# Two attention quads a pass over the array, rows through HBM, and the input norm on ScalarE, in a transformer sandwich on one core

## The reference

```python
def _taylor_softmax(x):
    t = 1.0 + x + 0.5 * x * x
    return t / jnp.sum(t, axis=-1, keepdims=True)

# _L0_attn_ref(x, ln_w, ln_b, w_q, w_kv, w_o, theta)
h = (x - mu) * jax.lax.rsqrt(var + EPS) * ln_w + ln_b
q = h @ w_q
kv = h @ w_kv
q, k, v = (to_heads(q), to_heads(k), to_heads(v))
q = _rope(q, theta); k = _rope(k, theta)
qk = jnp.einsum('bhkd,bhqd->bhkq', q, k) * scale
attn = _taylor_softmax(qk)
wv = jnp.einsum('bhkq,bhqd->bhkd', attn, v)
return wv.transpose(0, 2, 1, 3).reshape(B, T, DIMS) @ w_o

# _L0_ffn_ref(x, weight, bias): input and weight are rounded to a 6-bit grid, scaled by blocks of 32
xq, xs = _mx_quantize(x2)
wq, ws = _mx_quantize(w2)
out = xd @ wd.T + bias

# the whole
x = x + _layernorm(_L0_attn_ref(_layernorm(x, axis=-1), ...), axis=-1)
x = x + _layernorm(_L0_ffn_ref(_layernorm(x, axis=-1), ...), axis=-1)
```

## Time and profile before

| | |
|---|---|
| median of 3 runs | 648.65 us (647.7 to 649.6) |
| profiled execution | 651.11 us |
| its span, first to last instruction | 648.8 us |
| TensorE busy | 615.9 us, 95% |
| VectorE busy | 594.8 us, 92% |
| ScalarE busy | 530.0 us, 82% |
| GpSimd busy | 449.3 us, 69% |
| granted TensorE clock, mean | 0.985 |

### The profile page before, as it was taken

One profiled execution on the slowest core, in us unless ns is written; L12 is line 12 of the kernel. 1 busy time (PEld: TensorE's weight loads), 2 busy tenths in 40 slices (PEclk: granted clock), 3 DMA queues, 4 the chain that ended last, 5 costly groups with the idle time before them and its releaser, 6 DMA issues. The chain is left out here.

```text
span 648.8 us, 20724 instructions
## 1 busy us (share of the span) xinstructions
PE 615.9 (95%) x6620; PEld 457.7 (71%) x6620; DVE 594.8 (92%) x1489; ACT 530.0 (82%) x1448; POOL 449.3 (69%) x785
## 2 busy tenths in 40 slices
PE   6889999999999999999999999999999999999974
PEld 5666667676776776777777777767777766788763
DVE  5799899899899989999999999989999999987796
ACT  4347788888788897989888888978888888999973
POOL 3475466677777878788777867767877777765464
PEclk9699999999999999999999999999999999999996
DMA  7101031222223232232323232223223212230201
GB/s 245 34 2 42 20 76 30 72 63 65 50 72 88 70 91 68 75 84 67 62 67 83 77 86 73 69 57 101 60 68 92 76 39 41 68 91 18 68 26 49
DMA packets 52362, 43.51 MB, mean 67 GB/s; under 512 B 7201, under 2 KB 48545, under 8 KB 52257
## 3 DMA queue, kind: packets, MB, share of 16 engines
q1 hardware_dynamic: 51440, 41.42, 24.1%
q10 hardware_dynamic: 816, 0.79, 0.4%
HBM read 18.65 MB, written 8.39 MB: 42 GB/s over the span
## 5 line engine op out<-in xcount | busy, mean ns | idle before, releaser
L1168 ACT ACTIVATE feat<-ps_f 128x512 f32<-128x512 f32 x256 | 144.4, 599 | 4.9 <-PE ps_f L852 4.3
L691 DVE TENSOR_TENSOR kf<-kf 128x896 f32<-128x896 f32 (+1 forms) x128 | 131.2, 1027 | 1.8
L852 PE MATMUL ps_f<-qT,selr 128*128 128x512 f32 x320 | 122.1, 435 | 1.8 <-ACT qT L1236 1.3
L691 POOL TENSOR_TENSOR kf<-kf 128x224 f32<-128x224 f32 x64 | 76.5, 1195 | 13.3 <-DVE kf L1515 11.1
L1015 PEld LDWEIGHTS ps_mt<-kf,vp 128*32 128x32 f32 x2048 | 64.1, 110 | 30.0 <-issue 28.3
L1015 PE MATMUL ps_mt<-kf,vp 128*32 128x153 f32 x2048 | 79.7, 296 | 0.6 <-DVE kf L691 0.6
L1725 POOL TENSOR_TENSOR qsp<-kf,qsp 128x256 fp32r<-128x256 f32 x64 | 58.6, 916 | 9.8 <-ACT qsp L1259 9.6
L852 PEld LDWEIGHTS ps_f<-qT,selr 128*128 128x128 f32 x320 | 52.8, 190 | 15.2 <-issue 11.0
L913 PE MATMUL ps_o<-feat,main 120*32 120x512 f32 x448 | 59.7, 604 | 0.0
L916 PE MATMUL ps_o<-feat,rm 128*32 128x512 f32 x448 | 58.6, 593 | 0.0
L788 PE MATMUL ps_qk<-wkqv_h,hT_l 128*128 128x512 f32 x128 | 52.4, 409 | 3.3 <-DVE wkqv_l L1425 3.3
(11 more groups left out here) (199 smaller groups left out, 1885.2 us busy)
## 6 DMA issues: line engine op xcount, KB each, us to landing
xc<-L_attn_x SPq DMA_DIRECT2D x16, 512.0 KB, 4.5
result<-fin SPq DMA_DIRECT2D x64, 128.0 KB, 2.0
xa<-L_attn_x SPq DMA_DIRECT2D x15, 512.0 KB, 4.1
heads_out<-osb SPq DMA_DIRECT2D x224, 32.0 KB, 2.0
shares<-sums SPq DMA_DIRECT2D x112, 64.0 KB
sums<-osb SPq DMA_DIRECT2D x224, 2.0 KB
wkqv<-L_attn_w_kv ACTq DMA_DIRECT2D x2, 256.0 KB, 4.9
xa<-L_attn_x SPq DMA_DIRECT2D x1, 384.0 KB, 6.2
```

Source lines behind the costliest of these rows:

```text
L691: return eng.tensor_tensor(dims(row, F_MAIN, [[FW, heads], [HD, NR - 1], [1, HD]]), dims(row, F_LIN, [[FW, heads], [0, NR - 1], [1, HD]]), ...
L852: pe.matmul(ps_f[i % 2][:, :], selr[:, i], queries, start=True, stop=True).then_inc(sel_done, 1)
L1168: act.activation(feat[:, p2, i], ps_f[i % 2][:, :], ACT.Square).then_inc(squared, 1)
```

## The change

Five things are changed together.

- **Two quads at once.** `attend` now runs once for two quads, into two banks: `ps_o` and `ps_w`. The blocks that serve four heads are built from other columns of q (`fold_kq` puts them in another order): the fifth block of a quad now holds two heads of each of two quads, one quad in rows 0 to 63 and the other in rows 64 to 127. The products with `rm` are 64 rows deep instead of 128, those of one quad with the upper and those of the other with the lower half of the rows and in another bank. There are still four for a quad. `feat` still holds two tiles, which one pair now fills, so the first squares of a pair wait for the `attend` of the pair before. The linear layer moves from bank `ps_w` to bank `ps_qk`, which the projection of q and k also uses.
- **Rows through HBM.** `move_pair` writes two quads of `osb` to a buffer `rows` in HBM with one DMA; once both pairs are there, `fetch_heads` reads the denominators back with one and the heads with two; `store_inverses` writes the inverses with one, and `spread_shares` reads them with two. That is 8 DMAs a sequence (2, 3, 1 and 2) instead of 40.
- **The input norm on ScalarE.** `normalise_x` goes from VectorE to ScalarE; it needs `-mean/deviation`, which GpSimd makes in one more instruction a tile (`shift_x`).
- **Small ones.** `constant` and `rest_terms` are split in two stages each (`sum_linear`, `scale_terms`), with the same instructions. The turned weight of the linear layer goes through `ps_tr`.
- **A new order** for every engine, and 17 fillers (`fill`, two small matrix products of constants each) on TensorE in steps 1 to 47.

```diff
-    "tensor": (58, {
-        "attend": ((43, 54, 65, 76, 90, 101, 114, 127, 140, 154, 168, 183, 198,), (25, 39, 53, 69,), (474, 489, 503,
...
+    "tensor": (56, {
+        "attend": ((53, 72, 98, 123, 145, 170,), (38, 66,), (373, 402, 430, 459, 486, 515, 541, 567, 598, 622, 654, 682,
...
-        ps_o = bank("ps_o")
+        ps_o = [bank("ps_o"), ps_w]
...
-        rm = sb("rm", [P, 2, NQ, P])
+        rm = sb("rm", [P, 2, CH, HQ, VW])
...
+        rows = nc.dram_tensor("rows", [2, NQ, P, T], F32).ap()
+        inverses = nc.dram_tensor("inverses", [H * T // P, P], F32).ap()
...
-            def move_quad(t):
+            def move_pair(t):
 
-                par, quad, s = t.par, t.tile, t.seq
-                if quad == 0:
-                    wait(sp, norm_ready, NT * (s - 1))
-                    for tile in range(NT):
-                        wait(sp, shares_in[tile], 16 * CH * s)
+                par, quads = t.par, slice(t.tile - 1, t.tile + 1)
+                wait(sp, heads_in[par], 16 * CH * (t.load - 1))
+                wait(sp, sums_in, 16 * (t.seq - 1))
                 sp.wait_ge(o_copied, t.n)
-                for part in range(NT):
-                    sp.dma_start(sums[part * H + HQ * quad:part * H + HQ * (quad + 1)],
-                                 osb[HD:P:VW, par, quad, part * P:(part + 1) * P]).then_inc(sums_in, 16)
-                for h in range(HQ):
-                    row = HD * (HQ * (quad % 2) + h)
-                    sp.dma_start(heads_out[row:row + HD, par, quad // 2], osb[VW * h:VW * h + HD, par, quad]).then_inc(heads_in[par], 16)
+                sp.dma_start(rows[par, quads].rearrange("q r n -> r q n"), osb[:, par, quads]).then_inc(moved[par], 16)
+
+            def fetch_heads(t):
+
+                par, s = t.par, t.seq
+                wait(sp, inverses_out, 16 * s)
+                sp.wait_ge(moved[par], 16 * CH * t.load)
+                by_row = rows[par].rearrange("q (h r) n -> (q h) r n", r=VW)
+                sp.dma_start(sums[:, :], by_row[:, HD]).then_inc(sums_in, 16)
+                wait(sp, norm_ready, NT * (s - 1))
+                for c in range(CH):
+                    sp.dma_start(heads_out[:, par, c], by_row[c * HC:(c + 1) * HC, 0:HD]).then_inc(heads_in[par], 16)
+
+            def store_inverses(t):
+
+                s = t.seq
+                for c in range(CH):
+                    wait(sp, shares_in[c], 16 * s)
+                sp.wait_ge(inverted, s + 1)
+                sp.dma_start(inverses, sums[:, :]).then_inc(inverses_out, 16)
...
+            def add_main(t, out_, bank, p, j, feats, part, start):
+
+                pe.matmul(out_, main[0:NP, t.par, 2 * p + bank, VW * j:VW * (j + 1)], feat[0:NP, feats, 2 * bank + j % 2, part],
+                          start=start, stop=False, skip_group_check=True)
+
+            def add_rest(t, out_, bank, p, j, feats, part):
+
+                rows = slice(bank * P // 2, (bank + 1) * P // 2)
+                return pe.matmul(out_, rm[rows, t.par, p, j], feat[rows, feats, HQ, part],
+                                 start=False, stop=True, skip_group_check=True)
+
             def attend(t):
...
+                p = t.tile // 2
+                product_bank_is_free()
+                pe.wait_ge(rm_copied, t.seq + 1)
+                pe.wait_ge(squared, CHUNKS * t.n)
+                for bank in range(2):
+                    for j in range(HQ):
+                        add_main(t, ps_o[bank][VW * j:VW * (j + 1), :], bank, p, j, j // 2, slice(0, T), True)
+                for j in range(HQ):
+                    for bank in range(2):
+                        mm = add_rest(t, ps_o[bank][VW * j:VW * (j + 1), :], bank, p, j, j // 2, slice(0, T))
...
-                    wait(act, quad_done, t.n - 2)
+                    wait(act, quad_done, 2 * ((t.n - 1) // 2) if t.n <= BODY else max(BODY, t.n - 2))
...
+            def normalise_x(t):
+                act.wait_ge(x_centred, t.n)
+                wait(act, zT_done, t.n - 2)
+                act.activation(z[:, t.two, 0:D - 1], xa[:, t.par, t.tile, 0:D - 1], ACT.Identity,
+                               bias=centre_x[:, t.two:t.two + 1], scale=rs["x"][:, t.two:t.two + 1]).then_inc(z_ready, 1)
...
-            def normalise_x(t):
-                dve.wait_ge(rstd["x"], t.n)
-                wait(dve, zT_done, t.n - 2)
-                dve.tensor_scalar(z[:, t.two, 0:D - 1], xa[:, t.par, t.tile, 0:D - 1], mv[:, t.two, 0:1], rs["x"][:, t.two:t.two + 1],
-                                  ALU.subtract, ALU.mult).then_inc(z_ready, 1)
...
+            def shift_x(t):
+
+                pool.wait_ge(rstd["x"], t.n)
+                wait(pool, z_ready, t.n - 2)
+                pool.tensor_scalar(centre_x[:, t.two:t.two + 1], mv[:, t.two, 0:1], rs["x"][:, t.two:t.two + 1], -1.0,
+                                   ALU.mult, ALU.mult).then_inc(x_centred, 1)
```

681 lines of the change are left out of this document (356 added, 325 removed), and 98 rows, old and new, of the table ORDER.

## The result

The changed kernel takes 699.83 us (median of 4 runs, 695.73 to 705.62) where the kernel before takes 648.17 beside it (645.83 to 649.6): a ratio of 1.0807, 95% interval 1.0715 to 1.0899. The forecast was 628 us and faster; it was wrong by 72 us. The profiled execution took 697.35 us, its span is 695.6, the mean granted clock 0.972.

What follows compares the result with a forecast made beforehand. TensorE was taken as the bound. Span 648.8 - 24.1 (pairs) - 1.7 (tail) + 5 (coupling) = 628.0 us, other terms 0; expected median 628 us, 3.2% less, range 615 to 643.

Steps and rivals of the forecast that it cites:

- The bound: In the middle stretch TensorE bounds the kernel before, busy 472.96 of 480 us, with VectorE 3.4% behind.
- step 6: Hops through HBM: 6.1 us of landings against 4.8 us cover, VectorE's stall hidden, so 0, up to +18 us.
- The pair: In `attend`, eight half-depth `rm` products run side by side, saving 0.86 us a pair, 24.1 us on TensorE.
- The switch of shape: Changing the array's shape inside each pair costs 0.11 us, offset by fewer entries to attention: 0, ends -3 and +6.
- The tail: In the last stretch, halved `rm` blocks save 1.7 us (0 to 3.5).
- Coupling: Tighter order between engines raises TensorE's idle share from 1.5% to 2.5%: +5 us (0 to +13).
- SyncE's waits cost nothing: Behind SyncE's wait for `rows` stand loads and stores, which may be late without cost.
- Start and fillers: At the start, TensorE time of the fillers and clock won balance: 0 (-5 to +5).
- Rival 4: Late rows stall VectorE 3.7 us a sequence, making the kernel slower at 659 us; chance 0.05.
- Rival 1: VectorE is held up at the hops, unhidden, 1.3 us x 14 = 18 us: 646 at worst; chance 0.12.
- Rivals 2 and 3: ScalarE becomes the bound, 638 us, chance 0.08; half-depth products do not overlap, 652 or 649 us, chance 0.05.
- `rm` products in two groups 0.43 us apart: Sign in `attend` on TensorE: `rm` products starting in two such groups would make the forecast wrong.

Runs made afterwards that it cites:

- e15: Kernel before with the whole transfer route left out; reciprocal and normalisation read constants, output not the attention's: 640.72 us.
- e12: Changed kernel without the transfer route, and both banks' `rm` products read the same half of the rows, so they cannot run side by side: 676.67 us.
- e7: Changed kernel with the whole transfer route left out (rows, sums, heads, inverses, shares); reciprocal and normalisation read constants: 650.81 us.
- e14: Kernel before, instruction for instruction, with only the order on every engine reworked: 672.53 us.
- e17: Changed kernel without the transfer route; from the third tile on ScalarE normalises 32 of 255 columns: 651.07 us.
- e1: Changed kernel with all transfers made, but the attention's normalisation adds two constant tiles and waits for no transfer: 657.85 us.
- e2: Changed kernel with only SyncE's transfers reordered: input load behind the next sequence's first pair, first pair's heads fetched ahead of the denominators: 673.13 us.
- e9: Changed kernel without the transfer route and without the 17 fillers of TensorE's start: 652.15 us.

## Why the prediction was wrong, by its steps

1. **The bound.** Right for the kernel before: e15 takes away the waits at the route and TensorE is busy 478.92 of 480 us. It stopped being the bound in the changed kernel, by step 6.
2. **The pair, 24.1 us.** Right. The records show eight products side by side, and undoing this alone costs 25.9 us (e12), tail included; 24.1 + 1.7 had been predicted. The Trainium skill ("TensorEngine Tiling (Array Packing)", Tiling Modes) lists 64 by 32 as eight tiles that are independent; the trace agrees, with eight starts within 0.05 us.
3. **The switch of shape.** From `main` to `rm` 0.97 us pass (361.23 to 362.20) where from `main` to `main` 0.86 do: the 0.11 us taken from the kernel before. The Trainium skill ("TensorEngine Tiling (Array Packing)", Key Properties) says that a changed tiling mode drains the engine; the 0.11 us agree. That part stood in the working; taking 0 for the sum, because `attend` is entered and left half as often, was wrong. `attend` was mostly left without a switch before, as `sum_features` has 32 columns too, and a pair, 64 deep at its end, always leaves with one: its `rm` part takes 1.02 us, not 0.86. A pair takes 2.87 us where 3.54 - 0.86 = 2.68 would be free of new switches, 28 x 0.19 = 5.3 us: near the upper end of the bounds, +6.
4. **The tail, 1.7 us.** Within e12's 25.9; not measured by itself.
5. **Coupling, +5 us (0 to +13): a mis-sized term.** Without any route the kernel takes 650.8 us, not 628: the structure and order cost 23 us more than forecast, 28 in all. By the reciprocals, e7 against e15 (spans 650.1 and 638.9) loses 5.4 us ahead of the first reciprocal (88.0 against 82.6), and 4.0 behind the last one; between them it takes 476.0 us where e15 takes 474.2, while the pairs take 13 x 1.72 = 22.4 off, so 24 are lost there, 1.9 a sequence. The step put this at an idle share of TensorE going from 1.5% to 2.5%, of which e7 shows 2.3% in the middle (469.00 of 480). The share was right and the inference was not. Between their reciprocals e15 and then e7 show:

```profile
82.60:556.80 474.20, 473.12 (x4970) 347.70 (x4968) 456.11 (x1131) 414.10 (x1118) 362.78 (x607) 1.00 0.13 41
```

```profile
88.00:564.00 476.00, 465.11 (x4971) 333.50 (x4974) 447.81 (x1080) 429.57 (x1166) 375.25 (x655) 1.00 0.13 40
```

Idle time of TensorE grows from 1.1 to 10.9 us, 9.8 of the 24. The other 14 are busy time: 473.12 - 22.4 = 450.7 us were due, 465.11 are there. Some 5 of them are the switches of step 3. What the other 9 are made of, and what the idle time waits for, stays open. Over the whole program the linear layer's products, now into `ps_qk`, are busy for 100.5 us in e7 and 95.8 in e15, so 4.7 us can lie there; that move and the shared bank `ps_w` were not tried alone. The copies, the third tile of `feat`, the norm's length and the fillers are worth no more than 2.5 us each, taken one by one, and e14 shows that order alone can do as much. ScalarE's `z` took 606 ns and 38.8 us where 509 and 32.6 had been taken, but e17 shows that its length is worth nothing that can be told.
6. **The hops, 0 (up to +18): the step that failed.** It costed the way from the last copy to the reciprocal, 6.1 us against a cover of 4.8. That part was right in the main: the rows land in 3.0 us and the denominators in 2.2, 5.2 together, and VectorE waited 7.5 us in 7 sequences, 1.6 at most, where up to 1.3 in each had been taken. It never costed the way back, from the reciprocal to the first normalisation. There the change puts a transfer to HBM with a wait of SyncE ahead of the shares, two shares that the first tile needs both where it needed two of eight small ones, and the queue of heads and load in front. Without a wait the new order leaves 7.5 to 9.0 us from reciprocal to `att` (e1); it takes 9.0 to 12.7. In the kernel before the whole way from copy to `att` took 12.2 us in the eighth sequence (339.2 to 351.4, ahead of no wait) and 9.1 to 15.8 in all 14; in the changed kernel the shortest chain is an estimated 13.8 us, added up from the trace (2.9 for the rows, 2.2 for the denominators, 1.0 to the store of the inverses, 2.2 for these, 0.6 and 4.9 for the shares), and 14.0 at the least was seen ahead of a wait, while the order has room for 12.4 to 14.6 (e1, copy to `att` in its 14 sequences). Measured: 49 us in place of 0. Part of it is the clock: 0.98 in the middle and 0.76 in a stall, where e7 has 1.00 in the middle. By an estimate from these this is at most 480 x 0.02 = 10 us; how much was not separated.
   "SyncE's waits cost nothing" failed with it: behind the wait for the rows stand not only loads and stores but the inverses, and through them the shares. About half was the queue's order: e2 got 27 us back by that alone.
7. **Start and fillers, 0.** Nothing speaks against it: without the fillers +1.3 us (e9), too little to tell from no change. The first 40 us have a clock of 1.00 now, and yet the first reciprocal comes 2.6 us later than before.
8. **The rivals.** Rival 4 (slower, through late rows) had the right mechanism in kind, a stall of VectorE above its lead, with 3.0 us a sequence as the point from which it decides; the stalls were 44.9/14 = 3.2 us. But it had the stall at the reciprocal, not at the shares, and so a chance of 0.05. Rival 1 (the same stall, not hidden) looked at the same wrong place. Rivals 2 and 3 fell: ScalarE has the lowest busy time of the three in the middle (392.36 us, and without the route 433.42), and the half-depth products overlap. The signals named beforehand were good ones: TensorE under 95% in the middle (91%) was there. Others came out as misses: 40.3 us from reciprocal to reciprocal for about 35, and TensorE busy for 625.7 us for 589. "`rm` products in two groups 0.43 us apart" was badly put, since each block runs in two passes anyway: the two groups that show are passes of eight.

The sum in place of the forecast's: 628 + 23 (structure and order) + 49 (route) = 700, against 699.8 measured.

## What to carry to other kernels

A small value that goes out and comes back (a denominator and its inverse) is a round trip: write down every hop from the producer to the last consumer, with what stands ahead of each in its queue, and hold it against the distance that the order gives between those two instructions, in us. A route with fewer and larger transfers saves issue time on a queue that was not the bound and pays in latency; and a load of 512 KB must not stand ahead of a transfer for which an engine waits. Where the order of every engine is written by hand, a new one is worth tens of microseconds either way, so measure it with the change's parts taken out, and don't size its loss from an engine's idle share alone.
